# Adapter output products over three chunks of 128 rows in place of four pairs, and a reordered opening

## The reference

```python
x = x + einsum('bct,bcd->bdt', x, L0[i198]); x = x + einsum('bct,bcd->bdt', x, L1[i7])
x = x + einsum('bct,bcd->bdt', x, L2[i7]) + fside[i7][:, :, None]
lin(x, W, A, B) = x @ W + (x @ A[i7]) @ B[i7]
h = silu(lin(x, Wg, Ag, Bg)) * lin(x, Wu, Au, Bu)
x = x + lin(h, Wd, Ad, Bd)
```

## Time and profile before

| | us |
|---|---|
| three timed runs, median (lowest to highest) | 1347.47 (1345.93 to 1347.69) |
| the profiled execution | 1347.3 |
| its span, first to last instruction | 1345.5 |
| PE busy in the span | 1316.3 |
| DVE, ACT, POOL busy | 994.4, 549.2, 629.4 |
| mean granted clock of PE, share of full speed | 0.991 |

### The profile page before, as it was taken

How to read it: one execution, slowest core, us unless ns; L and a number is a source line. 1 busy time by engine, 2 the same in 40 slices (tenths; PEclk the granted TensorE clock), 3 DMA queues, 4 the chain that set the end, 5 groups by cost and what they waited for, 6 DMA issues and landing times.

```text
span 1345.5 us, 17990 instructions
## 1 busy us (share of the span) xinstructions
PE 1316.3 (98%) x6402; PEld 1095.5 (81%) x6402; DVE 994.4 (74%) x1530; ACT 549.2 (41%) x940; POOL 629.4 (47%) x531
## 2 busy tenths in 40 slices
PE   8699999999999999999999999999999999999998
PEld 7478888888888888888888888888887888888886
DVE  5776688777787667788678767777877876777765
ACT  3444444444334335444334334444433334433331
POOL 2256565455405545555431655554542444444440
PEclk8799999999999999999999999999999999999999
DMA  4445354445636334555383534444446432333321
GB/s 168 157 136 198 109 176 141 153 142 165 232 148 211 122 102 132 158 169 150 113 316 114 184 103 144 147 150 130 152 176 250 153 98 83 106 99 114 114 78 63
DMA packets 105687, 197.00 MB, mean 146 GB/s; under 512 B 10368, under 2 KB 54656, under 8 KB 105600
## 3 DMA queue, kind: packets, MB, share of 16 engines
q1 hardware_dynamic: 83328, 125.06, 28.6%
...
...
HBM read 160.69 MB, written 35.13 MB: 146 GB/s over the span
## 4 chain that ended last, share of the span: by engine, by line
PE 88%; DVE 6%; DMA 1%; POOL 1%; issue 1%; ACT 1%; SPq 0%; ACTq 0%; DVEq 0%; POOLq 0%
PE px L1104 26%; PE pd L1104 25%; PE py L1104 12%; PE pz L1104 6%; PE pv L1104 6%; PE pz L1120 4%; PE py L1120 2%; PE px L1120 2%; PE pd L1322 2%; DMA w_raw<-w_gu 1%; DVE wg_lo L844 1%; PE pd L1131 1%; DVE h_lo L1006 1%; DVE acc L1001 1%; PE pd L1177 1%
## 5 line engine op out<-in xcount | busy, mean ns | idle before, releaser
L496 POOL DMA_INDIRECT b_got<-b_table,idx_b x256 | 257.4, 1006 | 288.2 <-PE py L1120 204.5
L514 POOL TENSOR_TENSOR h_lo<-g,h_hi 128x512 fp32r<-128x512 f32 x128 | 176.4, 1378 | 334.0 <-ACT h_hi L586 332.8
L977 DVE TENSOR_TENSOR acc<-pd,acc 128x512 f32<-128x512 f32 x256 | 174.7, 690 | 82.1 <-PE pd L1104 81.7
L1104 PE MATMUL px<-xo_hi,wg_hi 128*128 128x512 f32 x544 | 222.9, 410 | 11.8 <-ACT g L586 5.7
L586 ACT ACTIVATE wg_hi<-w_raw 128x512 fp32r<-128x512 f32 (+1 forms) x272 | 155.6, 573 | 169.6 <-PE py L1120 94.5
L844 DVE TENSOR_TENSOR wg_lo<-w_raw,wg_hi 128x512 fp32r<-128x512 f32 (+1 forms) x272 | 198.1, 733 | 34.6 <-ACT wg_hi L586 33.8
L1104 PE MATMUL px<-xo_hi,wg_lo 128*128 128x512 f32 x544 | 213.5, 392 | 0.0
L1104 PE MATMUL px<-xo_lo,wg_hi 128*128 128x512 f32 x544 | 213.5, 392 | 0.0
L1104 PE MATMUL pd<-wd_hi,h_hi 128*128 128x512 f32 x512 | 203.1, 397 | 1.0 <-POOL h_lo L514 0.9
L1104 PE MATMUL pd<-wd_lo,h_hi 128*128 128x512 f32 x512 | 199.4, 389 | 0.0
L1104 PE MATMUL pd<-wd_hi,h_lo 128*128 128x512 f32 x512 | 199.3, 389 | 0.0
...
## 6 DMA issues: line engine op xcount, KB each, us to landing
w_raw<-w_gu SPq DMA_DIRECT2D x68, 512.0 KB, 3.7
...
xo_hi<-xops SPq DMA_DIRECT2D x21, 512.0 KB, 8.2
xo_lo<-xops SPq DMA_DIRECT2D x21, 512.0 KB, 9.9
...
```

Source lines behind the costliest of these rows:

```text
L496: gp.indirect_dma_start(out=dst, out_offset=None, in_=rows_of, in_offset=bass.IndirectOffsetOnAxis(ap=rows.bitcast(U32), axis=0)).then_inc ...
L514: return gp.tensor_tensor(dst, src_raw, src_hi, ALU.subtract)
L977: ins = dve.tensor_tensor(dst, pd[j][:, :], dst, ALU.add)
L1104: ins = pe.matmul(psum, w_parts[wi], x_parts[xi], start=(start and i == 0), stop=(stop and i == 2), skip_group_check=more)
```

## The change

A tile's eight samples now have three terms each, 48 rows, 384 rows in all, which are three chunks of 128. A chunk crosses samples: the three chunks touch 3, 4 and 3 samples, so `lora` issues three matmuls of 192, 256 and 192 columns in place of four of 128, and the samples at the chunks' edges are added up from two. `u` is 640 columns wide per tile, `b_got` has six slots, `select` runs 12 matmuls and three DVE operations (its third bank is pv or pd[2]), `selectors` is one operation, and the row numbers of the gathers (`block_numbers`) are worked out for chunks. Of the four combinations of high and low parts (of the token side and of B) the one of two low parts is left out.

The opening is reordered. Two small loads go on ACT's queue, SP waits before each large load; the warm-ups are (14, 4, 6, 2); `oe_add` comes before most picks, `o_combine(0)` after six; unit 0 of ACT and DVE is written out by hand, its copies between the high parts and its c11 and low parts in turn. In later units `weights_high(n+1, 0)` stands behind the S2 copy also in block 1; in unit -1 DVE's sums stand behind `u3`, and `weights_low(n+1, 3)` behind `select` and `finish`. Semaphore counts follow.

```diff
+HIGH_ORDER = (S1, A22, S2, S3, S4)
+LOW_ORDER = (S1, S2, S3, S4, A22)
+
+
+TERMS = 3
+SAMPLE_ROWS = TERMS * RANK
+CHUNKS = 3
+CHUNK_FROM = (0, 2, 5)
+CHUNK_SAMPLES = (3, 4, 3)
+U_FROM = (0, 3, 7)
+U_SAMPLES = 10
+U_COLS = U_SAMPLES * C
+
+
 PAIR_ORDER = (0, 4, 1, 5, 2, 6, 3, 7)
 PAIRS_FROM = 3
 TURNS_FROM = 5
-WARM_UP = (10, 14, 10)
+WARM_UP = (14, 4, 6, 2)
...
 
+        def select_bank(t, m, c):
+
+            banks = ((py, pz, pv), (pd[0], pd[1], pd[2]))[t]
+            if c < 2:
+                return banks[m][:, U_FROM[c] * C:(U_FROM[c] + CHUNK_SAMPLES[c]) * C]
+            n = CHUNK_SAMPLES[2] * C
+            return banks[2][:, m * n:(m + 1) * n]
+
+        def chunk(c):
+
+            n = CHUNK_SAMPLES[c] * C
+            return slice(U_FROM[c] * C, U_FROM[c] * C + n), slice(CHUNK_FROM[c] * C, CHUNK_FROM[c] * C + n)
+
         def finish_bank(q, t, j):
...
                              acc[:, q % 2, TP * t:TP * (t + 1), :]).then_inc(y_out[q % 2][t], 16)
 
             sp.dma_start(ints[:, 0, :], subject.partition_broadcast(P)).then_inc(ints_in, 16)
-            sp.dma_start(ints[:, 1, :], adapter.partition_broadcast(P)).then_inc(ints_in, 16)
             sp.dma_start(w2_four, w2_rows.rearrange("p (j n) -> p j n", j=TP)).then_inc(e0_in, 16)
             sp.dma_start(w1_four, w1_pairs.rearrange("p (j n) -> p j n", j=TP)).then_inc(e0_in, 16)
-            sp.dma_start(bias_src, bias_pairs).then_inc(bias_in, 16)
+
+            sp.wait_ge(ints_in, 2 * 16)
+            sp.wait_ge(e0_in, 2 * 16)
             load_x(0, 0)
+            sp.wait_ge(pick_made, TP)
             load_weights(0)
             load_x(0, 1)
...
 
-            def gather_b(q, m, t, pairs=range(TP)):
-                for j in pairs:
-                    p = TP * t + j
-                    gather_rows(raw(b_got[:, p, :]), b_table[m], idx_b[:, q * QP + p:q * QP + p + 1], b_got_in[t])
+            def gather_b(q, m, t, chunks=range(CHUNKS)):
+                for c in chunks:
+                    gather_rows(raw(b_got[:, CHUNKS * t + c, :]), b_table[m], idx_b[:, c, 2 * q + t:2 * q + t + 1],
+                                b_got_in[t])
 
             def gather_pair(q, i):
...
-            act.wait_ge(consts, 3)
+            act.dma_start(ints[:, 1, :], adapter.partition_broadcast(P)).then_inc(ints_in, 16)
+            act.dma_start(bias_src, bias_pairs).then_inc(bias_in, 16)
...
                              turn_banks[j][:, :].rearrange("p (k c n) -> p k c n", k=2, c=2)).then_inc(o_a2_kept, 1)
-            for k, summed in ((S1, o_s1_sum), (S2, o_s2_sum), (S3, o_s3_sum), (S4, o_s4_sum)):
+
+            def keep_s1(n):
+                act.wait_ge(p1_mm, n + 1)
+                copy(g0[:, :], px[:, :]).then_inc(s1_kept, 1)
+
+            def keep_s5(n):
+                act.wait_ge(p5_mm, n + 1)
+                copy(up1[:, :], py[:, :]).then_inc(s5_kept, 1)
+
+            def keep_s2(n):
+                act.wait_ge(p6_mm, n + 1)
+                copy(up0[:, :], px[:, :]).then_inc(s2_kept, 1)
+
+            def sum_high(k, summed):
                 act.wait_ge(summed, 2 if k == S1 else TP)
-                copy(xo_hi[:, k, :], s_raw[k]).then_inc(o_hi[k], 1)
-            copy(xo_hi[:, A22, :], a2_raw[1]).then_inc(o_hi[A22], 1)
+                copy(xo_hi[:, k, :], s_raw[k]).then_inc(o_hi, 1)
 
             def v_high(q, t):
                 act.wait_ge(v_masked, 2 * q + t + 1)
...
 
+
+            sum_high(S1, o_s1_sum)
+            keep_s1(0)
+            copy(xo_hi[:, A22, :], a2_raw[1]).then_inc(o_hi, 1)
+            sum_high(S2, o_s2_sum)
+            keep_s5(0)
+            sum_high(S3, o_s3_sum)
+            keep_s2(0)
+            sum_high(S4, o_s4_sum)
+            ua_high(0, 0, 0)
+            weights_high(1, 0)
+            act.wait_ge(p2_mm, 1)
+            weights_high(1, 1)
+            ua_high(0, 1, 1)
+            ua_high(0, 0, 1)
+            b_high(1)
+            weights_high(1, 2)
+            act.wait_ge(p4_mm, 1)
+            copy(g1[:, :], px[:, :]).then_inc(c21_kept, 1)
+            ua_high(0, 1, 0)
+            weights_high(1, 3)
+
             for q, b in units():
                 n = unit(q, b)
                 last = n + 1 == QUARTERS * UNITS
+                if n == 0:
+                    continue
                 if b % 2 and b >= 1:
                     B = q * BLOCKS + b - 1
...
-                elif q:
-                    act.wait_ge(h_lo_done[0], blocks_done(q, -1))
-                copy(g0[:, :], px[:, :]).then_inc(s1_kept, 1)
-                act.wait_ge(p5_mm, n + 1)
                 if b == 0:
                     act.wait_ge(ua_done, 4 * q + 4)
-                elif n:
+                else:
+                    act.wait_ge(h_lo_done[0], blocks_done(q, b - 1))
+                keep_s1(n)
+                if b:
                     act.wait_ge(h_done[1], blocks_done(q, b - 1))
-                copy(up1[:, :], py[:, :]).then_inc(s5_kept, 1)
-                if not last and b > 0:
+                keep_s5(n)
+                if not last and b > 1:
                     weights_high(n + 1, 0)
-                act.wait_ge(p6_mm, n + 1)
-                if b != 0 and n:
+                if b:
                     act.wait_ge(h_done[0], blocks_done(q, b - 1))
-                copy(up0[:, :], px[:, :]).then_inc(s2_kept, 1)
-                if not last and b <= 0:
+                keep_s2(n)
+                if not last and b <= 1:
                     weights_high(n + 1, 0)
                 j = turn_at(q, b)
                 if j is not None:
...
                                   ).then_inc(idx_done, 1)
 
             def block_numbers():
+
                 dve.tensor_scalar(p_int[:, 1:2], p0, 4, None, ALU.logical_shift_right)
-                dve.tensor_scalar(p_int[:, 3:4], p0, 5, 1, ALU.logical_shift_right, ALU.bitwise_and)
                 dve.tensor_scalar(r_int2[:, :], r_int[:, :], 15, None, ALU.bitwise_and)
-                link(dve.tensor_scalar(p_int[:, 4:5], p0, 15, None, ALU.bitwise_and))
+                link(dve.tensor_copy(c_place[:, :, :], c_int[:, :, :]))
                 dve.tensor_copy(p_f[:, 0:1], p_int[:, 1:2])
-                link(dve.tensor_scalar(p_f[:, 2:3], p_int[:, 3:4], float(P), None, ALU.mult))
-                link(dve.tensor_tensor(p_f[:, 3:4], p_f[:, 2:3], p_int[:, 4:5], ALU.add))
-                dve.tensor_scalar(idx_b[:, :], pair_ad[:, :], float(RANK), p_f[:, 3:4], ALU.mult, ALU.add
-                                  ).then_inc(idx_b_done, 1)
+                link(dve.tensor_scalar(c_mask[:, :, :], c_place[:, :, :], 0.0, None, ALU.is_ge))
+                link(dve.scalar_tensor_tensor(c_mask[:, :, :], c_place[:, :, :], float(SAMPLE_ROWS), c_mask[:, :, :],
+                                              ALU.is_lt, ALU.mult))
+                link(dve.tensor_tensor(c_place[:, :, :], c_place[:, :, :], c_mask[:, :, :], ALU.mult))
+                link(dve.tensor_reduce(c_row[:, :], c_place[:, :, :], AX.X, ALU.add))
+                by_tile = adf[:, :].rearrange("p (t s) -> p t s", s=2 * TP)
+                link(dve.tensor_tensor(
+                    c_tmp[:, :, :, :], by_tile.unsqueeze(1).to_broadcast([P, CHUNKS, 2 * QUARTERS, 2 * TP]),
+                    c_mask[:, :, :].unsqueeze(2).to_broadcast([P, CHUNKS, 2 * QUARTERS, 2 * TP]), ALU.mult))
+                ins = dve.tensor_reduce(c_ad[:, :, :], c_tmp[:, :, :, :], AX.X, ALU.add)
+                for c in range(CHUNKS):
+                    dve.tensor_copy(u_mask[:, U_FROM[c]:U_FROM[c] + CHUNK_SAMPLES[c]],
+                                    c_mask[:, c, CHUNK_FROM[c]:CHUNK_FROM[c] + CHUNK_SAMPLES[c]])
+                link(ins)
...
+                    dve.wait_ge(sel_mm, 2 * q + t)
+                dve.tensor_tensor(
+                    sel[:, :, :].rearrange("p k (s e) -> p k s e", e=SAMPLE_ROWS),
+                    pattern[:, :, :].unsqueeze(2).to_broadcast([P, 2, 2 * TP, SAMPLE_ROWS]),
+                    onehot[:, first:first + 2 * TP].unsqueeze(1).unsqueeze(3).to_broadcast([P, 2, 2 * TP, SAMPLE_ROWS]),
+                    ALU.mult).then_inc(sel_done, 1)
 
 
             dve.memset(es_four, 0.0)
-            dve.wait_ge(consts, 2)
...
             link(ins)
-            for p in range(TP):
-                picks(p)
+            picks(0)
             dve.wait_ge(e2_done, 1)
             dve.wait_ge(oe_mm, 1)
             dve.tensor_tensor(es_four[:, :, C:2 * C], four(pv[:, 0:TP * C]), e2_four, ALU.add).then_inc(oe_add, 1)
-            for p in range(TP, QP - 1):
+            for p in range(1, TP + 2):
                 picks(p)
             picked(0)
-            picks(QP - 1)
-            sums(0)
+            for p in range(TP + 2, QP):
+                picks(p)
             dve.wait_ge(eb_done, 1)
             o_combine(0)
+            sums(0)
             picked(1)
             block_numbers()
             for g in (0, 2, 1, 3):
                 weights_low(0, g)
             dve.wait_ge(eb_done, 2)
             o_combine(1)
```

(68 more changed lines are left out.)

170 lines of the change are left out of this document (100 added, 70 removed).

## The result

| | before | after |
|---|---|---|
| median (lowest to highest), us | 1347.24 (1345.93 to 1347.69) | 1324.6 (1324.0 to 1325.16) |
| ratio, 95% interval | | 0.9833 (0.9816 to 0.9850) |
| profiled execution, span | 1347.3, 1345.5 | 1325.06, 1323.3 |

The change saves 22.6 us, 1.7%. The forecast was 1311 with 1300 to 1322 as its range, so the sign was right and the size was not: about 14 us of the forecast gain are missing, and the time lies outside the range.

A forecast was written before the change was run, and what follows sets the result against it. The prediction took TensorE's (PE's) matmul stream to bound the body, with waits and a half clock in the opening. From 1347.3 us: -12.0 (opening) -0.85 (quarter 0) -24.0 (`lora`) +0.3 (quarters) = 1310.7, forecast 1311, range 1300 to 1322.

The forecast's parts named there:

- `lora`: Adapters' output products: weight loads 0.11 us apart set the pace; 0.107 us saved a call, 24.0 us over 56 blocks.
- C: Rival for `lora`: the weight load hides behind the longer matmuls, 0.174 us saved a call, time 1296; chance 0.03.
- D: Rival for `lora`: 192 columns run at the f32 rate, 256 at the product's, no saving, time 1335; chance 0.05.
- E: Rival for `lora`: all columns run at the f32 rate, 0.10 us more a call, time 1362; chance 0.03.
- The opening: To block 0's first product: 6.0 us gained to `o_layers(1)`, 8.0 after it; the walk's 14 taken as 12.
- Rival A: Opening: the clock falls again, gain 7 us in place of 12, time 1316; chance 0.15.
- Quarter 0: Block 0 there is bound by the DVE and ACT string; 0.85 us gained of the 1.8 that PE saves.
- The changes of quarter: At each of three, the savings of `select`, `lora` and waits are paid back: +0.1 us each, +0.3 in the sum.
- (a): Block 1 at a change of quarter: `weights_high(n+1, 0)` behind `keep_s2` takes away the 0.7 us wait on ACT's `up`.
- (b): Unit -1: `u3` ahead of the four sums; PE starts `select(q, 0)` about 1.4 us later, ends it 0.9 later.
- (c): Unit -1: `weights_low(n+1, 3)` behind `select` and `finish`; next `w_raw` load issued at about 393.3 us, 387.39 before.
- B's bound: Rival B: the changes of quarter keep their gains, 3.5 us each, 10.5 in all, time 1300; chance 0.12.

The follow-up runs named there:

- experiment 7: Against the changed kernel with (b) and (c) undone, `lora` calls with one matmul, three of 128 columns, or three of 256: 1259.51, 1307.85, 1312.25 us, one execution each.
- experiment 4: Against the changed kernel with (b) and (c) undone, (a) undone as well: 1313.9 us, ratio 0.9762.
- Experiment 5: Against the changed kernel, in block 0 of each quarter the second tile's first adapter product takes tile 0's `u` and rows: 1322.31 us, ratio 0.9823.

## Why the prediction was wrong, point by point

**`lora`, right in kind, 15% too high (24.0 forecast, 20.8 measured).** The mechanism is the forecast one: the weight load paces these matmuls, and width hides behind it. The row method gives for the call after what was forecast. The kernel after, PE's timeline about one call:

```profile
63.26 0.39 PE L1227 MATMUL pz<-xo_hi,wg_lo 128*128 128x512 f32 x1
63.49 0.48 PE L1244 MATMUL pz<-u,b_got 128*128 128x192 f32 x3
63.81 0.41 PE L1227 MATMUL px<-xo_hi,wg_hi 128*128 128x512 f32 x1
64.06 0.39 PE L1227 MATMUL px<-xo_lo,wg_hi 128*128 128x512 f32 x1
```

From 63.26 to 64.06 it is 0.80 us, 0.91 before; less two products 0.35, as forecast. Yet the block saves 0.37 us in four calls, 0.093 a call and not 0.107. The step that failed is that the call's neighbourhood was taken as the whole block. Width does cost a little (experiment 7: 0.07 us a block, 0.018 a call). With it the block comes out: 4 x 0.11 - 0.07 = 0.37, where 0.11 is a matmul of 128 columns (the eight of experiment 7 at 0.93 us are 768 columns wider in all, worth 0.05; the rest is 0.11 each). Why the row beside the call doesn't show this cost is open. Over 56 blocks it makes the 3.2 us, beside two items that cancel. At block 3 of quarter 0 PE now waits 1.3 us for POOL's low part of h (0.5 before); the prediction called POOL's side worth nothing. And block 5 of quarter 1, 0.7 us longer than its like before, no longer is.

Rivals C, D and E are out: C by the 0.116 us that a matmul costs, D and E by a 256-wide call that costs what a 192-wide one does. `select` is close to the forecast on PE: its 12 matmuls stand 0.11 to 0.14 apart, and at full clock a call takes 1.43 us where it took 1.81, 0.38 less for 0.43. On DVE its operations have 448, 448 and 384 columns, not three of 384 (0.61, 0.61 and 0.55 us), 0.1 us more a call than counted.

**The opening, 5.5 us too high.** The half to block 0 was right to 0.3 us. The half to `o_layers(1)` came out at 33.19 for 25.4, 7.8 us late; the 2 us that the forecast had taken off its walk hide a part of that. It failed at one step: "`o_layers(0)` starts at about 18" (24.56 measured), which has `o_combine(0)` start right behind the six picks, near 15, and puts no time on the gathers that it reads. In the kernel before the fourth of them landed at 18.1, 5.8 us after its issue. The change issues it at 11.52, 0.8 us earlier (the first is 1.1 earlier, for 1.5 to 2 forecast), so by the same 5.8 us it would land at 17.3 (an estimate from these two rows), 2 us after the picks' end. The other 2 us of the 4.25 us wait fit the second thing not asked: the change moves 2 MB of large loads from before the gathers into their midst. With these held back the fourth lands at 13.8, and `o_layers(0)` starts at 17.57, the forecast's 18. The rest is the clock: from `o_combine(0)` to the end of `o_layers(0)` takes 11.3 us in the changed kernel and 6.3 with the gathers first.

Rival A foresaw the half clock and a price for it (7 in place of 12; 6.5 measured, 6.5 to 9.5 over the nine kernels with this opening) but looked for it between 36 and 50 us; it came some twenty microseconds earlier, in a wait that A didn't name. Its argument against, "no single wait over 2 us", rested on a reading that is too coarse. The prediction tied the 0.50 of the kernel before to the 4.6 us wait. A narrow stretch of that kernel has the fall already in progress at 46.0, while the products behind the 2.71 us wait still run (the last of them starts at 45.75):

```profile
45.50:45.90 0.40, 0.40 (x3) 0.19 (x1) 0.40 (x2) 0.17 (x1) 0.40 (x1) 1.00 0.27 103
45.90:46.10 0.20, 0.20 (x2) 0.00 (x0) 0.20 (x1) 0.20 (x1) 0.20 (x1) 0.69 1.43 246
```

And the kernel with all three reorderings undone loses its clock behind a wait of 1.31 us:

```profile
15.20:16.50 1.30, 0.00 (x0) 0.00 (x0) 1.12 (x2) 0.00 (x0) 0.99 (x2) 1.00 1.01 348
16.50:20.00 3.50, 3.50 (x17) 3.50 (x17) 2.15 (x6) 0.26 (x1) 0.46 (x1) 0.50 1.02 354
```

The Trainium skill ("TensorE: Matmul & The Clock Gate", HAM oscillation) has long gaps return the clock to half; the 4.25 us wait agrees, but it does not tell which of the shorter waits, 1.31 to 2.7 us here, are followed by a fall; for 1.78 and for 2.3 to 2.4 us the runs show both.

**Quarter 0, 1 us too high.** The string of DVE and ACT was said to bind block 0 and let half the saving through. It lets nothing through: one of PE's two waits on ACT's `g` grew from 1.1 to 1.5 us, and the two blocks took 0.2 us longer.

**The changes of quarter, 4.65 us too low.** All of (a), (b) and (c) happened as told. (a) removed its wait, worth 1.0 us each and not 0.7 (experiment 4). (b) starts `select(q, 0)` 14.2, 14.2 and 14.5 us after unit -1's start where it was 12.8, so 1.4 to 1.6 us later (1.4 forecast; PE's wait of 1.8 to 2.1 is longer, because PE gets there 0.46 earlier). The load is issued 20.5, 20.2 and 20.65 us after unit -1's start (20.1 forecast), but the sums begin at 24.65, 24.56 and 24.87, not at 23.8 (397.0 - 373.2): the load takes 4.2 to 4.3 us to DVE's start, where 3.7 was taken, the median of all. That is 0.8 to 1.1 us, which the string hands on: most of the 1.1 and 1.3 us missed at the first and third change. And the string reaches PE one step earlier than told: the small waits on the `u` of `select(q, 0)` are gone, as forecast, but a new one stands at the `u` of `select(q, 1)` (3.9 us in all), and those forecast at block 1 (0.5 and 1.4 us) aren't there. Experiment 5 shows that this is no second cost. What had no place in the sum is the clock: after a wait of about 2 us it can fall in the body as well, 1.1 us net at the second change. The prediction read 1.00 from 100 to 1330 us and took the body to be safe; but there the longest wait was 0.7 us.

**What the prediction priced and did not weigh.** It worked out that (b) and (c) eat the savings of `select`, `lora` and the waits at each change, and stopped there. The measured price of the two together is 13 us (1324.6 to 1311.55; 12.2 of it at the changes of quarter), more than half of what the whole change gains. B's bound, 3.5 us kept at each change, is 2.2 to 2.5 in truth (50.4 to 47.9 and 48.15).
